# Five of sixteen mask-by-place products of a graph kernel moved from VectorE to GpSimd

## The reference

```python
h = jnp.maximum(_layernorm(x, axis=-1), 0.0)
x = x + _L0_gnn_ref(h, adj, L0_gnn_W, L0_gnn_a, L0_gnn_gamma, L0_gnn_beta)
h = jnp.maximum(_layernorm(x, axis=-1), 0.0)
x = x + _L1_gnn_ref(h, adj, ...)
h = jnp.maximum(_layernorm(x, axis=-1), 0.0)
x = x + _L2_gnn_ref(h, adj, ...)
h = jnp.maximum(_layernorm(x, axis=-1), 0.0)
x = x + _L3_gnn_ref(h, adj, L3_gnn_W, L3_gnn_a)
```

## Time and profile before

| | us |
|---|---|
| median of 3 runs | 1516.84 |
| lowest and highest | 1514.72, 1520.01 |
| the profiled execution's own time | 1518.37 |
| its span in the profile | 1516.6 |
| DVE busy in the span | 1229.1 (81%) |
| POOL busy | 917.0 (60%) |
| TensorE's matmuls busy | 952.2 (63%) |

### The profile page before, as it was taken

One profiled execution on the slowest core, in us unless ns is written; L12 is line 12 of the kernel. 1 busy time (PEld: TensorE's weight loads), 2 busy tenths in 40 slices (PEclk: granted clock), 3 DMA queues, 4 the chain that ended last, 5 costly groups with the idle time before them and its releaser, 6 DMA issues.

```text
span 1516.6 us, 16874 instructions
## 1 busy us (share of the span) xinstructions
PE 952.2 (63%) x4667; PEld 671.9 (44%) x4667; DVE 1229.1 (81%) x1599; ACT 821.5 (54%) x2858; POOL 917.0 (60%) x885
## 2 busy tenths in 40 slices
PE   1027655762599895488899966566616647656572
PEld 0014422321478785477788832222206647632230
DVE  7889677997699999999999348999867998846461
ACT  2025543668176665176686727658974557643220
POOL 2042278721786896189777548886546776437881
PEclk9998887886799998699999988777856767879786
DMA  9961376521222231001110044533115544247666
GB/s 331 240 222 54 91 229 186 167 82 49 91 70 77 78 108 58 30 22 51 48 50 29 15 135 136 145 105 98 55 61 158 178 130 128 71 145 210 181 196 157
DMA packets 101574, 176.89 MB, mean 117 GB/s; under 512 B 47488, under 2 KB 56224, under 8 KB 99424
## 3 DMA queue, kind: packets, MB, share of 16 engines
q0 software_dynamic: 31472, 102.93, 23.2%
q1 hardware_dynamic: 67280, 72.13, 15.2%
q10 hardware_dynamic: 2720, 0.68, 0.2%
HBM read 145.78 MB, written 34.10 MB: 119 GB/s over the span
## 4 chain that ended last, share of the span: by engine, by line
POOL 35%; DVE 21%; issue 19%; PE 12%; ACT 6%; DMA 5%; POOLq 0%; DVEq 0%; SPq 0%; ACTq 0%
POOL big L723 15%; POOL big L696 15%; PE PS L1379 3%; PE PS L1353 2%; ACT big L983 2%; PE PS L1334 2%; DVE big L1664 2%; DVE big L1600 2%; DVE big L1781 2%; DVE big L1785 2%; DMA big<-tab,SI 2%; DMA big<-in_adj 1%; PE PS L1417 1%; POOL big L745 1%; DVE big L1769 1%
## 5 line engine op out<-in xcount | busy, mean ns | idle before, releaser
L723 POOL TENSOR_TENSOR big<-big 128x512 f32<-128x512 f32 x373 | 376.7, 1043 | 160.2 <-DVE big L1742 145.2
L983 ACT ACTIVATE big<-big 128x64 f32<-128x64 f32 x1496 | 371.0, 338 | 153.8 <-DVE big L1742 147.1
L1785 DVE TENSOR_REDUCE big<-big 128x32 f32<-128x2048 f32 (+4 forms) x126 | 297.7, 2362 | 4.3
L1334 PE MATMUL PS<-big,ident 128*128 128x512 f32 x348 | 186.5, 694 | 119.5 <-DVE big L1769 60.4
L1353 PE MATMUL PS<-ident,big 128*128 128x128 f32 x1740 | 232.5, 294 | 38.4 <-POOL big L723 30.7
L1353 PEld LDWEIGHTS PS<-ident,big 128*128 128x128 f32 x1740 | 218.3, 154 | 47.8 <-issue 23.2
L696 POOL DMA_INDIRECT big<-tab,SI x142 | 176.6, 1244 | 78.5 <-issue 39.6
L1777 DVE TENSOR_TENSOR big<-big,PS 128x2048 f32<-128x2048 f32 (+4 forms) x84 | 198.5, 2363 | 17.5 <-PE PS L1365 14.6
L1334 PEld LDWEIGHTS PS<-big,ident 128*128 128x128 f32 x348 | 74.9, 223 | 221.2 <-issue 200.5
L696 POOL DMA_INDIRECT big<-h_rows,SI x142 | 137.4, 968 | 47.6 <-issue 28.4
L1350 PE MATMUL PS<-big,ident 128*128 128x512 f32 x174 | 103.8, 757 | 61.0 <-POOL big L723 56.5
(11 more groups left out here) (182 smaller groups left out, 1598.8 us busy)
## 6 DMA issues: line engine op xcount, KB each, us to landing
big<-in_adj SPq DMA_DIRECT2D x16, 1024.0 KB, 6.1
tab<-big SPq DMA_DIRECT2D x64, 132.0 KB, 1.8
big<-tab SPq DMA_DIRECT2D x32, 264.0 KB, 3.2
h_rows<-big SPq DMA_DIRECT2D x32, 256.0 KB, 2.0
big<-h_rows SPq DMA_DIRECT2D x32, 256.0 KB, 2.9
big<-in_x SPq DMA_DIRECT2D x16, 256.0 KB, 5.1
big<-xs SPq DMA_DIRECT2D x4, 1024.0 KB, 9.3
h_table<-big SPq DMA_DIRECT2D x16, 256.0 KB, 2.1
```

Source lines behind the costliest of these rows:

```text
L723: ins = pool.tensor_tensor(bd(wbuf[:, i % NWB, j, :]), bd(rows[:, k + j, :]), over_d(S[:, h, k + j, :], B), ALU.mult)
L983: ins = act.activation(to, row, ACT.Copy, scale=S[:, h, k + j, b:b + 1])
L1334: mm = pe.matmul(to.rearrange("p (b d) -> p b d", b=B), ident[:, :], rows[:, k, :].rearrange("p (b c) -> p b c", b=B)[:, :, 0:D], start=(k ...
L1785: run(dve.tensor_reduce(scores(u, t)[:, h, k:k + n, :].rearrange("p k b -> p (k b)"), bd(prod[:, 0:n * E]), AX.X, ALU.add))
```

## The change

The products of tiles 5, 7, 9, 11 and 13 are made by GpSimd, by the same instruction, into a buffer of their own: pool_ranked, the place of spread, which is no longer needed when places is made. A product there waits until DVE has taken the four maxima of the one before it (list_taken), and DVE waits for the product ahead of its first maximum (list_ranked). The products of tiles 5 and 7 stand in GpSimd's program ahead of the transfers of part 0, those of tiles 9, 11 and 13 behind these and ahead of the transfers of part 1. DVE keeps the other eleven.

```diff
+RANKED_BY_POOL = {0: [5, 7], 1: [9, 11, 13], 2: []}
+BY_POOL = [c for part in range(len(INFO_PARTS)) for c in RANKED_BY_POOL[part]]
...
+        pool_ranked = spread.rearrange("p t j -> p (t j)")
...
+            def rank_list(i):
+
+                if i == 0:
+                    pool.wait_ge(places_made, 1)
+                    pool.wait_ge(places_cast, 1)
+                else:
+                    pool.wait_ge(list_taken, i)
+                pool.tensor_tensor(pool_ranked, mask[:, BY_POOL[i], :], places, ALU.mult).then_inc(list_ranked, 1)
...
             for part in range(len(INFO_PARTS)):
+                for c in RANKED_BY_POOL[part]:
+                    rank_list(BY_POOL.index(c))
                 send_info(part)
...
             for c in range(NT):
-                run(dve.tensor_tensor(ranked, mask[:, c, :], places, ALU.mult))
+                if c in BY_POOL:
+                    ranks = pool_ranked
+                    dve.wait_ge(list_ranked, BY_POOL.index(c) + 1)
+                else:
+                    ranks = ranked
+                    run(dve.tensor_tensor(ranked, mask[:, c, :], places, ALU.mult))
                 for q in range(4):
-                    run(dve.max(cand[:, 0, q * 8:(q + 1) * 8], ranked[:, q * (N // 4):(q + 1) * (N // 4)]))
+                    ins = dve.max(cand[:, 0, q * 8:(q + 1) * 8], ranks[:, q * (N // 4):(q + 1) * (N // 4)])
+                    if c in BY_POOL and q == 3:
+                        tell(ins, list_taken, BY_POOL.index(c) + 1)
+                    else:
+                        run(ins)
```

More of the change, by code:

```diff
@@ L307, in program @@
         places_cast = sem("places_cast")
+        list_ranked = sem("list_ranked")
+        list_taken = sem("list_taken")
         lists_made = sem("lists_made")
```

## The result

The changed kernel is slower: 1523.84 us median of 6 runs (1520.54 to 1526.15) against 1515.38 of 6 (1514.53 to 1520.01). The ratio is 1.0049 with a 95% interval of 1.003 to 1.0067, so it is 0.3 to 0.7% slower, which lies inside the forecast range (1519.5 to 1536) and 4 us under the point of 1528. The profiled execution has a span of 1521.0 us.

What follows compares the result with a forecast made beforehand. DVE's list loop was taken to bound the kernel from 111.8 to 172 us. Up to tile 7 -0.05, tile 9 +7.99, tiles 10 to 13 +2.30 - 1.26 + 3.03 - 1.26 gave +10.75 us: 1528, range 1519.5 to 1536.

Steps and rivals of the forecast that it cites:

- What bounds: Between 111.8 and 172 us DVE's list loop alone sets the time; a microsecond there is one of the kernel.
- what happens ahead of end_row 0 is swallowed: Before 111.8 us, DVE's gains or losses first meet the first end_row's 2.33 us wait for ScalarE.
- The savings: Five products of 1.26 us leave DVE, 6.3 us; four lie on the path and are worth 5.0 us.
- The price of a product: GpSimd's dense f32 products, 0.453 us at 128 elements and 1.276 at 512, extended to 2048: 4.57 us.
- T: Time of one 128x2048 16-bit product on GpSimd, taken as 4.57 us, bounded by 2.3 and 6.
- The wait at tile 9: GpSimd's product stands behind eight info transfers until 134.4, so DVE idles 9.25 us; 7.99 net of the product saved.
- The holds: DVE's products of tiles 4, 6, 10, 12 held until GpSimd's running product ends: 1.74, 1.21, 2.30, 3.03 us.
- The tail doesn't cushion: After the loop, row 14's 4.66 us wait is no slack; 171.89 to 184.44 moves as a block with the loop's end.
- A quick product: Rival: 16 bits halve GpSimd's product time to 2.3 us; +2.7 us, 1519.6, result not slower; 10%.
- No hold: Rival: GpSimd doesn't hold DVE's 16-bit products, only the tile 9 wait remains; +4.2 us, 1521.0; 8%.
- A slow product: Rival: GpSimd's product takes 6 us or more for 16-bit conversion; +18 us and above, 1535 and more; 9%.
- the change does what it is meant to: Rival: GpSimd is ready each time and nothing is held; -5.0 us, 1511.8; 3%.

Runs made afterwards that it cites:

- run of nine: Against the kernel before: GpSimd makes the products of tiles 6 to 14 in one double-buffered run ahead of all info transfers, two parts; 1504.8 us, ratio 0.9926.
- the quarters: Against the changed kernel: each GpSimd product cut into four of 128x512 that follow without a wait; 1522.94 us.
- the unused products: Against the changed kernel: DVE makes all sixteen products, GpSimd makes its five at the same queue places and nobody uses them; 1520.67 us, ratio 1.0027.
- the run converted early: Against the kernel before: GpSimd makes tiles 6 to 13 in one run, all in part 0, with the three old parts kept; 1508.59 us, ratio 0.9951.

## Why the prediction was right, and what was off

- **What bounds.** The reading that DVE's loop is the path between 111.8 and 172 us was right: in nine kernels the loop moved by -12 to +7.5 us and the whole time with it, as far as the runs can tell. That what happens ahead of end_row 0 is swallowed fits too: tile 4's product was held 1.24 us in the change, and end_row 0 still waited 3.10 us for ScalarE.
- **The savings.** 1.26 us a product on the path, as worked out; nine of them are 11.3 us, and with 0.7 for the conversion they are the 11.98 of the run of nine.
- **The price of a product: the term that was mis-sized.** I took T = 4.57, it is 4.06. The step was to draw the line through the dense f32 products; in 16 bits a product of 128x512 takes 1.11 us (start to start in the quarters, 142.41 to 143.52), not 1.276, and the slope to 2048 is (4.06 - 1.11) / 1536 = 1.92 ns an element instead of 2.14. My own working with T = 4.06 gives +8.2 instead of +10.75, for T enters it five times (tile 9 once, the holds of tiles 10 and 12 once each, that of tile 6 twice). From the median of 1515.38 that is 1523.6 for a measured 1523.84. That it comes so near is luck, since the interval of the runs is 5.6 us wide; the loop says +7.46, and the 0.7 between is the transfers and tile 6, below.
- **The wait at tile 9.** Predicted 9.25, measured 8.28: about 0.5 of it is T, and the rest that the eight transfers took 10.18 us (121.57 to 131.75) instead of 10.74, as one fewer of them was stretched.
- **The holds.** Predicted 1.74, 1.21, 2.30 and 3.03; measured 1.24, 0, 1.76 and 2.49. Three are short by the 0.5 of T alone. The one at tile 6 needed GpSimd to be busy at DVE's coming. With the shorter product my working would still have it held 0.2 us; but end_row 0 waited 3.10 us for ScalarE and not the 2.4 of that working, so DVE came 0.43 us after GpSimd had ended.
- **The tail doesn't cushion.** Right in that the end of the loop went on to the load of SI; wrong in that this piece moves as a block. The load of SI:

```profile
189.77 0.45 SPq L553 DMA_DIRECT2D SI<-info  x1
```

  I had forecast about 195 for it, from 184.44. The 5.3 us between are the loop's 7.46, less 0.85 by which end_row 0 came earlier in this trace (110.24 instead of 111.09), less 1.28 by which the piece from end_row 12 to the load was shorter (11.27 instead of 12.55). The last goes with the time of TensorE's matmuls (see the end). Behind the first gather the span is 1327.1 us instead of 1328.2, as long as before to 0.1%.
- **The rivals.** A quick product: between it and the forecast, T at 4.06 is far nearer the latter. No hold: excluded by the unused products and by the 2.98 and 3.71. A slow product: excluded by the 4.06. That the change does what it is meant to: excluded by the 8.28.
- **What the text didn't see.** It listed DVE's products as what GpSimd holds, and missed the conversions. In the change none coincides with a product, so it cost nothing there; in two experiments it cost 3.2 us.

## What to carry to other kernels

Work given to GpSimd costs what stands ahead of it in GpSimd's queue, not only its own duration: here one product behind eight transfers took 7 us of the 7.5. Beside GpSimd's products, a DVE product with two SBUF inputs (up to 4.15 us instead of 1.22) and an f32 tensor_scalar between SBUF tiles (3.44 instead of 0.23) stood still until GpSimd was done, so look at what DVE runs beside the moved work, instruction by instruction. Give GpSimd a whole run of consecutive steps, double-buffered, such that DVE has none of these beside it, and put the transfers behind the run if what follows them leaves time for it, as here: the same idea then turned from 0.5% slower to 0.7% faster.

## What the runs showed of the hardware

- A GpSimd tensor_tensor of 128x2048 in 16 bits takes 4.06 us, 3.3 times DVE's 1.22; four of 128x512 take 4.46.
- What was held beside a GpSimd product, and what not: a DVE tensor_scalar of 128x128 f32 took 3.44 us instead of 0.23, a tensor_tensor of 128x2048 f16 up to 4.15 instead of 1.22. MAX8 and an end_row with one input in PSUM were never held, and a memset on GpSimd held none of DVE's products. The hold goes both ways: where DVE's product got in at a boundary, the next GpSimd one was held in its turn (two products 9.08 us instead of 8.12, two quarters 3.28 instead of 2.2).
- The tail from end_row 12 to the first gather goes with TensorE's granted clock. Busy times by window: of the kernel before, of the changed one, and of the run converted early (window, length, busy us of PE, PEld, DVE, ACT, POOL, then granted clock, DMA share, GB/s):

```profile
171.89:188.37 16.48, 9.95 (x40) 6.83 (x40) 4.54 (x13) 6.03 (x13) 1.93 (x2) 0.71 0.36 92
```

```profile
178.50:193.92 15.42, 8.73 (x40) 5.77 (x40) 4.54 (x13) 5.91 (x13) 1.94 (x3) 0.84 0.40 105
```

```profile
165.48:179.39 13.91, 7.29 (x40) 5.17 (x40) 4.54 (x13) 5.91 (x13) 1.93 (x2) 0.96 0.49 133
```

A window with the same 40 matmuls lasts 16.5 us at a mean granted clock of 0.71, 15.4 at 0.84 and 13.9 at 0.96 (1 is the upper of its two levels, 2.4 GHz, throughout); over all ten profiles the order by clock is only rough, as one at 0.89 took 15.3. By TensorE's busy time it is close: in each of the ten the window is 6.5 to 6.7 us longer than the time of its matmuls (7.3 to 10.0 us), so nearly the whole difference lies in these. What sets the clock there was not tried. That is up to 2.7 us (13.8 to 16.6) that no edit of this study aimed at, and it is one reason why single profiles of these kernels should be compared by the loop and not by their spans.
